# First self-attention's weight transposes ahead of the next rows, and six sign-MLP tiles split ahead of the last rows

## The chip, the core and the metric

The kernel runs on one core of a Trainium2 chip. The core has a matrix engine (TensorE, PE in the rows; PEld is its weight load), a vector engine (VectorE, DVE), a scalar engine (ScalarE, ACT), a general engine (GpSimd, POOL) and a queue that issues transfers (SyncE, SP). The engines run side by side and wait for one another by semaphores. The metric is the device time of one launch in microseconds, the median of several executions.

## What is computed

The reference takes x of 16 x 64 rows by 512 and runs two layers of three blocks, each block on the layer norm of x and added to it. Only the two blocks that the change touches are shown, cut to what matters.

```python
def _L0_attn_ref(x, Wq, bq, Wk, bk, Wv, bv, Wp):        # 16 heads of 32, groups of 64 tokens
    q = (x @ Wq + bq).reshape(Bb, Nn, H, D)
    k = (x @ Wk + bk).reshape(Bb, Nn, H, D)
    v = (x @ Wv + bv).reshape(Bb, Nn, H, D)
    q = jnp.einsum('bnhe,ei->bnhi', q, Wp)
    k = jnp.einsum('bnhe,ei->bnhi', k, Wp)
    scores = jnp.einsum('bnhi,bmhi->bnhm', q, k) / math.sqrt(D)
    attn = jax.nn.softmax(scores, axis=-1)
    return jnp.einsum('bnhm,bmhe->bnhe', attn, v).reshape(Bb, Nn, E)
...
def _L0_ffn_ref(x, k0, k1, k2, s0, s1, s2):             # weights are +1 or -1
    h = jnp.concatenate([x, -x], axis=-1)
    h = jax.nn.relu(s0 * _conn_dense(k0, h)) * 2        # 512 (as 1024) -> 2048
    h = jax.nn.relu(s1 * _conn_dense(k1, h)) * 2        # 2048 -> 2048
    return s2 * _conn_dense(k2, h)                      # 2048 -> 512
...
x = x + _L0_attn_ref(_layernorm(x, axis=-1), ...)
x = x + _L0_ffn_ref(_layernorm(x, axis=-1), ...)
```

## The kernel before

Every engine has its own program, written out by hand in the order in which it runs; nothing reorders it. A wait at the head of an engine's queue holds all that stands behind it there.

**First self-attention** (`head_attention`). The 1024 rows are eight tiles of 128. A turn handles two tiles (256 rows), so there are four turns, i = 0 to 3; the turns 1 and 2 are the body of a hardware loop, 0 and 3 are written apart. In turn i TensorE does in this order: the key projections and the query projections (`project_transposed`, three products of high and low halves: hi by hi, lo by hi, hi by lo; L941), scores of the first tile (L957), transposes of the rows that the sign MLP will read (`transpose_signs`, L932), values of the first tile (L948), scores of the second tile, values of the second tile, transposes of the next turn's normalised rows (`transpose_x`, L925), then for the softmax weights four batches of four transposes (`transpose_weights(i, s, n)`, tile s, half n of the heads, L966) with the weighted values (`attend`, L976) of tile 0 after the third batch and those of tile 1 after the fourth.

Around them: ScalarE takes the exponentials out of the score banks (`exponentials(i, s, n)`, eight activations of 64 columns each, L1033), copies the transposed next rows (`copy_x`, L1027, x_xT_hi) and the first tile's values (L1067). VectorE takes the negative maxima (L1104, s_nmax), copies the second tile's values (L1171, s_v_diag), copies the transposed weights out of their two banks (`copy_weights`, L1109, s_pT), makes the low half of the next rows (`split_x`, L1099, x_xT_lo), scales and adds the result (`attended`, L1113, L1116, L1121), and takes the statistics of rows. The weight transposes write the banks 4 and 5, the same as the key projections and the sign transposes; a batch for tile 1 waits until the batch of tile 0 in the same bank was copied (`pT_ok`). The next turn's projection waits for both halves of the next rows (`xhi_ok`, `xlo_ok`). VectorE also expands one chunk of the sign MLP's first weights in each turn (L1152), and GpSimd adds the output bias to the rows in the same stretch (L1230).

**Sign MLP.** The rows go in two halves of 512. In the first layer TensorE makes 16 hidden tiles of 128 x 512, eight matmuls each (L2079), into two banks in turn. ScalarE takes each through the ReLU (L2124) into one of two float32 buffers, and VectorE splits a buffer into its float16 high half (L2178) and low half (L2180) (`split_hidden`). ScalarE's tile n waits until tile n-2 is split; TensorE's tile n waits until ScalarE has read tile n-2. The first half of the rows comes from the turns 0 and 1. The last two row tiles (turn 3) are normalised here: VectorE aggregates the statistics (L2130), GpSimd makes the reciprocal deviation (L2217, L2219), VectorE makes f_xn (L2134), and TensorE transposes them after the whole first layer of the first half (L2087). GpSimd expands the second layer's weights (L2227, f_w), one piece after hidden tiles 3, 7, 11 and 15 and later one for each tile.

## Time and profile before

| what | value |
|---|---|
| three executions | 1104.45, 1107.32 and 1108.89 us, median 1107.32 |
| the profiled execution, its own time | 1112.53 us |
| its span in the trace | 1110.7 us |
| TensorE busy, share of the span | 1066.0 us, 96% |
| VectorE, ScalarE, GpSimd | 58%, 31%, 19% |
| mean granted clock of TensorE | 0.985 |
| first self-attention, turns 0 to 3 | 176.3 to 291.4 us |
| sign MLP, first layer of the first half | 291.4 to 324 us |

Times in the rows are from the span's start. A timeline row gives start, duration, engine, line, operation, output and inputs, the form, how many instructions of a kind stand in a row (x8: from the first's start to the last's end), and in brackets the engine's idle time before with what released it. A matmul's end is modelled, so a row of TensorE can overlap the next. Where the row ends an idle time in "issue", the engine waited for nothing that the profile shows.

### The profile page before, as it was taken

How to read it: one execution, taken by the hardware profiler on the slowest of the kernel's cores; microseconds unless marked ns; L12 is line 12 of the kernel's file. 1: busy time of each engine (PE TensorE's matmuls, PEld its weight loads, DVE VectorE, ACT ScalarE, POOL GpSimd, SP SyncE). 2: the span in 40 equal slices, each digit the busy share in tenths (PEclk: the TensorE clock that was granted, in tenths of full speed). 3: DMA queues.
4: the chain of work that ended last, by engine and by line, in shares of the span. 5: the costliest groups of instructions: out<-in, count | busy, mean ns of one | idle time of the engine just before them, and what ended most of it. 6: DMA issues, size and time to landing. Idle time of an engine off the chain costs nothing.

```text
span 1110.7 us, 16819 instructions
## 1 busy us (share of the span) xinstructions
PE 1066.0 (96%) x6165; PEld 664.2 (60%) x6165; DVE 641.2 (58%) x1114; ACT 347.2 (31%) x984; POOL 208.9 (19%) x202
## 2 busy tenths in 40 slices
PE   7999989999899999999999999999889999999897
PEld 4566648888444444444444466657679687887433
DVE  2454345787666732256762174457865947569677
ACT  1232235666530000130001042236232514225534
POOL 0111101333122222000001611132414122140002
PEclk9999989999999999999999999999999999999898
DMA  9976902000024591014536469963000000021105
GB/s 338 387 255 219 354 20 76 2 1 23 26 93 146 177 19 20 0 53 155 179 119 222 168 217 372 366 240 113 1 1 1 1 0 0 1 108 59 58 1 76
DMA packets 68593, 129.59 MB, mean 117 GB/s; under 512 B 9408, under 2 KB 13504, under 8 KB 68160
## 3 DMA queue, kind: packets, MB, share of 16 engines
q1 hardware_dynamic: 67680, 127.38, 35.2%
q0 software_dynamic: 864, 1.57, 1.1%
q8 instruction: 29, 0.48, 0.2%
q14 instruction: 20, 0.16, 0.0%
HBM read 120.92 MB, written 8.01 MB: 116 GB/s over the span
## 4 chain that ended last, share of the span: by engine, by line
PE 72%; issue 11%; DVE 8%; POOL 4%; SPq 2%; DMA 2%; ACT 1%; POOLq 0%; DVEq 0%; ACTq 0%
PE bank L2079 24%; PE bank L449 5%; PE bank L2106 5%; PE bank L419 4%; PE bank L941 4%; PE bank L380 3%; PE bank L2307 3%; PE bank L948 2%; PE bank L1562 2%; PE bank L1631 2%; PE bank L2342 2%; PE bank L494 2%; PE bank L483 2%; PE bank L469 2%; DMA xres<-in_x_dram 2%
## 5 line engine op out<-in xcount | busy, mean ns | idle before, releaser
L2124 ACT ACTIVATE f_act<-bank,f_sgn 128x512 f32<-128x512 f32 x64 | 44.0, 687 | 267.8 <-PE bank L2079 262.2
L2079 PE MATMUL bank<-f_a_lo,f_w 128*128 128x512 f16 x512 | 115.7, 379 | 0.0
L2079 PE MATMUL bank<-f_a_hi,f_w 128*128 128x512 f16 x512 | 115.7, 379 | 0.0
L2079 PEld LDWEIGHTS bank<-f_a_lo,f_w 128*128 x512 | 50.1, 98 | 60.4
L2079 PEld LDWEIGHTS bank<-f_a_hi,f_w 128*128 x512 | 50.1, 98 | 60.2
L2178 DVE CAST f_b_hi<-f_act 128x512 f16<-128x512 f32 x32 | 28.4, 887 | 95.0 <-ACT f_act L2124 85.6
L1838 DVE TENSOR_TENSOR s_e<-s_pair,s_tables 128x512 f32<-128x512 f32 x64 | 41.4, 689 | 42.8 <-POOL s_kT L1914 15.4
L419 PE MATMUL bank<-x_cT,x_qT 128*64 128x512 f32 x256 | 62.9, 637 | 0.0
L449 PE MATMUL bank<-x_cN,x_eT 128*64 128x512 f32 x256 | 56.9, 596 | 0.0
L1823 DVE TENSOR_TENSOR s_k_diag<-s_kT,s_spread 128x512 f32<-128x512 f32 x64 | 48.8, 819 | 1.6 <-PE bank L1587 1.6
L1720 ACT ACTIVATE s_e<-bank,s_nmax 128x64 f32<-128x64 f32 x128 | 38.1, 338 | 35.5 <-DVE s_nmax L1783 35.4
L2227 POOL TENSOR_SCALAR f_w<-f_upper_bits 128x2048 bf16<-128x2048 uint8 x16 | 30.9, 1932 | 82.1 <-PE bank L2079 82.1
L711 DVE TENSOR_TENSOR x_aT_lo<-bank,x_aT_hi 128x512 fp32r<-128x512 f32 x16 | 11.1, 692 | 60.8 <-ACT x_aT_hi L574 60.8
L744 POOL TENSOR_TENSOR x_mv<-x_mv,eps 128x2 f32<-128x2 f32 x10 | 1.9, 194 | 214.9 <-DVE x_mv L606 214.9
L1033 ACT ACTIVATE s_e<-bank,s_nmax 128x64 f32<-128x64 f32 x128 | 38.3, 351 | 4.1 <-DVE s_nmax L1104 4.0
L1587 PE MATMUL bank<-s_k_diag,s_qT 128*64 128x256 f32 x256 | 34.2, 401 | 4.8 <-DVE s_k_diag L1823 4.0
L419 PEld LDWEIGHTS bank<-x_cT,x_qT 128*64 128x64 f32 x256 | 18.0, 145 | 34.6 <-issue 34.3
L449 PEld LDWEIGHTS bank<-x_cN,x_eT 128*64 128x64 f32 x256 | 17.6, 137 | 32.8 <-issue 32.6
L2079 PE MATMUL bank<-f_xT_hi,f_w 128*128 128x512 f16 x128 | 33.8, 387 | 3.2 <-ACT f_act L2124 3.2
L1913 POOL TENSOR_TENSOR s_kT<-s_e 128x256 f32<-128x256 f32 x16 | 13.3, 831 | 115.8 <-DVE s_e L1838 115.8
L390 PE MATMUL bank<-x_kw,x_qw 128*128 128x512 f32 x64 | 30.5, 637 | 4.2 <-DMA x_kw<-in_x_kw_dram 4.2
L751 POOL MEMSET x_ones<- 128x128 f32 x1 | 0.2, 205 | 180.6 <-DMA x_bk<-in_x_kb_dram 180.6
(339 smaller groups left out, 2300.2 us busy)
## 6 DMA issues: line engine op xcount, KB each, us to landing
x_cT<-in_ctx_cols_dram SPq DMA_DIRECT2D x32, 1024.0 KB, 8.9
x_cN<-in_ctx_rows_dram SPq DMA_DIRECT2D x32, 1024.0 KB, 11.5
f_upper_bits<-in_f_w_dram SPq DMA_DIRECT2D x20, 256.0 KB, 3.9
f_row<-in_f_wg_dram SPq DMA_DIRECT2D x11, 256.0 KB, 3.7
f_long_row<-in_f_wd_dram SPq DMA_DIRECT2D x4, 704.0 KB, 6.2
f_row<-in_f_wu_dram SPq DMA_DIRECT2D x11, 256.0 KB, 2.7
f_part<-in_f_wgT_dram SPq DMA_DIRECT2D x8, 352.0 KB, 3.4
f_part<-in_f_wuT_dram SPq DMA_DIRECT2D x8, 352.0 KB, 3.3
```

The lines of the kernel that those rows point to most:

```text
L380: mm = pe.matmul(bank[Q_BANK[half]][:, a * PT:(a + 1) * PT], l[:, k, c * P:(c + 1) * P], r[:, k, :], start=(m == 0 and k == 0), stop=(m == ...
L419: mm = pe.matmul(bank[S_BANK[s]][SEQ * b:SEQ * (b + 1), :], qT[:, k, tokens], cT[s][:, b, k, :], start=(k == 0), stop=(k == KC - 1))
L449: mm = pe.matmul(bank[AV_BANK[s]][SEQ * b:SEQ * (b + 1), :], eT[s][:, k, SEQ * b:SEQ * (b + 1)], cN[s][:, b, k, :], start=(k == 0), stop=( ...
L941: mm = pe.matmul(bank[banks[g]][:, a * PT:(a + 1) * PT], l[:, k, c * P:(c + 1) * P], r[:, k, :], start=(m == 0 and k == 0), stop=(m == 2 a ...
L1033: ins = act.activation(e_sb[s][n][:, j * SEQ:(j + 1) * SEQ], bank[S_BANK[s][n]][:, j * SEQ:(j + 1) * SEQ], ACT.Exp, bias=nmax[s][:, h:h + ...
L1587: mm = pe.matmul(at[SEQ * b:SEQ * (b + 1), cols], qT[:, g, a, tokens], k_diag[g % 2][:, a, b, :], start=False, stop=(a == AB - 1), skip_gr ...
L1720: ins = act.activation(e_sb[n][:, j * SEQ:(j + 1) * SEQ], bank[S_BANK[s][n]][:, j * SEQ:(j + 1) * SEQ], ACT.Exp, bias=nmax[s][:, h:h + 1], ...
L1823: ins = dve.tensor_tensor(k_diag[g % 2][:, a, :, :].rearrange("p b (j n) -> p b j n", j=4), kT[:, g, a, s * P:(s + 1) * P].rearrange("p (b ...
L1838: ins = dve.tensor_tensor(flat(prods[t]), flat(pair[:, :, :]), table(t), ALU.mult)
L2079: mm = pe.matmul(h_bank[s][:, :], weights(2 * i + s, k), part[:, k, cols], start=(n == 0 and k == 0), stop=(n == 1 and k == k_chunks - 1))
L2106: mm = pe.matmul(y_bank[t % 2][:, :], part[:, k, t * P:(t + 1) * P], w2_sb[:, k, :], start=(n == 0 and k == 0), stop=(n == 1 and k == HC - 1))
L2124: act.activation(act32[s][:, :], h_bank[s][:, :], ACT.Relu, scale=sgn[:, layer % 2:layer % 2 + 1]).then_inc(h_read, 1)
```

## The change

In the first self-attention, TensorE transposes tile 0's weights (two batches) before it transposes the next turn's rows; the wait for the low half of the rows (`xlo_ok`) moves from the head of the key projection to its third product. ScalarE does the second tile's second half of exponentials before it copies the next rows. VectorE copies tile 0's two weight batches before the second tile's values, and all four batches before it splits the next rows. In the sign MLP, VectorE splits the first six hidden tiles of the first half before it normalises the last two row tiles; the loop over the tiles then begins at pair 3. Each engine runs as many instructions of each kind as before, apart from the loop's own.

```diff
-            def project_transposed(banks, hi, lo, done):
+            def project_transposed(banks, hi, lo, done, split=None):
                 for g in range(2):
                     for a in range(2):
                         c = 2 * g + a
                         for m, (l, r) in enumerate(((hi, xT_hi), (lo, xT_hi), (hi, xT_lo))):
+                            if split is not None and c == 0 and m == 2:
+                                pe.wait_ge(xlo_ok, split)
                             for k in range(KC):
...
                 pe.wait_ge(xhi_ok, 2 * (FIRST + i) + 2)
-                pe.wait_ge(xlo_ok, 2 * (FIRST + i) + 2)
-                project_transposed(K_BANK, wk_hi, wk_lo, k_done)
+                project_transposed(K_BANK, wk_hi, wk_lo, k_done, 2 * (FIRST + i) + 2)
                 project_transposed(Q_BANK, wq_hi, wq_lo, q_done)
...
                 project_values(1)
-                if not last:
-                    pe.wait_ge(e_ok, 4 * i + 2)
-                    transpose_x(i + 1)
                 if not first:
                     pe.wait_ge(flo_ok, 2 * i)
                 transpose_weights(i, 0, 0)
                 transpose_weights(i, 0, 1)
+                if not last:
+                    pe.wait_ge(e_ok, 4 * i + 2)
+                    transpose_x(i + 1)
                 transpose_weights(i, 1, 0)
...
                 exponentials(i, 1, 0)
+                exponentials(i, 1, 1)
                 if not last:
                     copy_x(i + 1)
-                exponentials(i, 1, 1)
...
                 negative_maxima(i, 1, 1)
+                copy_weights(i, 0, 0)
+                copy_weights(i, 0, 1)
                 dve.wait_ge(v_done, 2 * i + 2)
...
                 ins.then_inc(v1_ok, 1)
-                copy_weights(i, 0, 0)
-                copy_weights(i, 0, 1)
                 copy_weights(i, 1, 0)
+                copy_weights(i, 1, 1)
                 if not last:
                     split_x(i + 1)
-                copy_weights(i, 1, 1)
                 attended(i, 0)
...
-            dve.wait_ge(rstd_ok, 2)
-            for s in range(2):
-                dve.tensor_scalar(xn[s][:, :], xres[:, TILES - 2 + s, :], mv[:, s, 0:1], rstd[:, s:s + 1],
-                                  ALU.subtract, ALU.mult).then_inc(xn_ok, 1)
+            def normalise_last():
+                dve.wait_ge(rstd_ok, 2)
+                for s in range(2):
+                    dve.tensor_scalar(xn[s][:, :], xres[:, TILES - 2 + s, :], mv[:, s, 0:1], rstd[:, s:s + 1],
+                                      ALU.subtract, ALU.mult).then_inc(xn_ok, 1)
...
-                        with dve.Fori(0, HC // 2) as i:
+                        ahead = 0
+                        if half == 0:
+
+                            ahead = 3
+                            for n in range(2 * ahead):
+                                split_hidden(first, n, n % 2, hi, lo)
+                            normalise_last()
+                        with dve.Fori(ahead, HC // 2) as i:
```

What stands in a row on VectorE at the end of turn 0 (turns 1 and 2 alike), before:

```order
L1104 TENSOR_REDUCE s_nmax<-bank 128x8 x2
L1171 COPY s_v_diag<-bank 64x8x32 x4
L1109 COPY s_pT<-bank 128x512 x3
L1099 TENSOR_TENSOR x_xT_lo<-bank,x_xT_hi 128x4x128 x2
L1109 COPY s_pT<-bank 128x512
L1113 RECIPROCAL s_total<-s_total 128x16
```

And after:

```order
L1105 TENSOR_REDUCE s_nmax<-bank 128x8 x2
L1110 COPY s_pT<-bank 128x512 x2
L1174 COPY s_v_diag<-bank 64x8x32 x4
L1110 COPY s_pT<-bank 128x512 x2
L1100 TENSOR_TENSOR x_xT_lo<-bank,x_xT_hi 128x4x128 x2
L1114 RECIPROCAL s_total<-s_total 128x16
```

Two weight copies moved ahead of the values' copies, and the low halves moved behind the last weight copy.

TensorE at the end of turn 0, from the second tile's values on, before:

```order
L948 MATMUL bank<-x_m_hi,x_xT_lo 128x512 x4
L925 MATMUL bank<-ident,x_xn 128x128 x8
L966 MATMUL bank<-ident,s_e 128x128 x12
L976 MATMUL bank<-s_v_diag,s_pT 64x64 x16
L966 MATMUL bank<-ident,s_e 128x128 x4
L976 MATMUL bank<-s_v_diag,s_pT 64x64 x16
```

And after:

```order
L950 MATMUL bank<-x_m_hi,x_xT_lo 128x512 x4
L968 MATMUL bank<-ident,s_e 128x128 x8
L925 MATMUL bank<-ident,x_xn 128x128 x8
L968 MATMUL bank<-ident,s_e 128x128 x4
L978 MATMUL bank<-s_v_diag,s_pT 64x64 x16
L968 MATMUL bank<-ident,s_e 128x128 x4
L978 MATMUL bank<-s_v_diag,s_pT 64x64 x16
```

The eight transposes of tile 0's weights stand ahead of the eight of the next rows.

VectorE at the start of the sign MLP, before:

```order
L2130 BN_AGGR f_mv<-stats 128x2 x2
L2134 TENSOR_SCALAR f_xn<-xres,f_mv,f_rstd 128x512 x2
L2201 UNCONDITIONAL_BRANCH
L2201 ISA
L2178 ISA
L2178 COPY f_a_hi<-f_act 128x512
```

And after (the pair of rows at L2180 and L2182 stands there six times; one is shown):

```order
L2131 BN_AGGR f_mv<-stats 128x2 x2
L2180 CAST f_a_hi<-f_act 128x512
L2182 TENSOR_TENSOR f_a_lo<-f_act,f_a_hi 128x512
...
L2136 TENSOR_SCALAR f_xn<-xres,f_mv,f_rstd 128x512 x2
L2210 UNCONDITIONAL_BRANCH
L2210 ISA
L2180 ISA
```

The two row tiles f_xn moved behind six splits, which now stand outside the loop.

## Rows read from the trace of the kernel before

**Rows 1.** Windows: stretch, length, busy times of PE PEld DVE ACT POOL, clock, DMA.
```profile
233.50:262.50 29.00, 27.87 (x252) 23.54 (x248) 23.40 (x46) 18.39 (x84) 10.44 (x8) 1.00 0.00 0
...
291.40:324.00 32.60, 29.41 (x132) 12.97 (x129) 24.53 (x42) 10.31 (x15) 8.26 (x6) 0.95 0.10 24
...
303.00:304.00 1.00, 1.00 (x4) 0.36 (x3) 0.88 (x3) 0.00 (x0) 0.00 (x0) 0.50 0.00 0
```

**Rows 2.** Timeline, all engines, end of turn 2 and start of turn 3.
```profile
256.08 1.73 DVE L1171 COPY s_v_diag<-bank 64x256 f32<-64x256 f32 x4 [1.29 <-PE bank L948]
...
256.92 1.11 ACT L1027 CAST x_xT_hi<-bank 128x512 fp32r<-128x512 f32 x2
257.85 1.29 DVE L1109 COPY s_pT<-bank 128x512 f32<-128x512 f32 x2
...
259.90 0.42 ACT L1033 ACTIVATE s_e<-bank,s_nmax 128x64 f32<-128x64 f32 x1
259.96 1.28 DVE L1099 TENSOR_TENSOR x_xT_lo<-bank,x_xT_hi 128x512 fp32r<-128x512 f32 x2
...
260.46 0.42 PEld L966 LDWEIGHTS bank<-ident,s_e 128*128 128x128 f32 x4 [0.21 <-ACT s_e L1033]
...
261.16 0.69 DVE L1109 COPY s_pT<-bank 128x512 f32<-128x512 f32 x1
...
262.52 0.54 PEld L941 LDWEIGHTS bank<-x_xT_hi,s_wk_hi 128*128 128x128 f32 x4
```

**Rows 3.** Timeline, the middle of turn 2, where VectorE and GpSimd meet.
```profile
243.33 4.57 POOL L1230 TENSOR_TENSOR xres<-xres,s_out_bias 128x512 f32<-128x512 f32 x2
243.48 3.29 DVE L1152 TENSOR_TENSOR f_w<-f_upper_bits,f_lower_bits  x1
...
246.69 1.39 DVE L1104 TENSOR_REDUCE s_nmax<-bank 128x8 f32<-128x512 f32 x2
...
247.40 0.32 ACT L1033 ACTIVATE s_e<-bank,s_nmax 128x64 f32<-128x64 f32 x1 [1.20 <-DVE s_nmax L1104]
```

**Rows 4.** Timeline, end of turn 0: the transposes' issue and the last weight copy.
```profile
197.73 1.02 PEld L925 LDWEIGHTS bank<-ident,x_xn 128*128 128x128 f32 x8
...
203.23 0.68 DVE L1109 COPY s_pT<-bank 128x512 f32<-128x512 f32 x1
```

**Rows 5.** Timeline, end of turn 3.
```profile
285.14 1.73 DVE L1171 COPY s_v_diag<-bank 64x256 f32<-64x256 f32 x4 [1.37 <-PE bank L948]
...
288.14 1.28 ACT L2112 ACT_TABLE_LOAD   x1
...
290.08 0.69 DVE L1109 COPY s_pT<-bank 128x512 f32<-128x512 f32 x1 [0.98 <-PE bank L966]
```

**Rows 6.** Timeline, first layer of the sign MLP, from its start to its end.
```profile
291.44 0.55 PEld L2079 LDWEIGHTS bank<-f_xT_hi,f_w 128*128 x4
...
295.71 0.25 DVE L2130 BATCH_NORM_AGGREGATE f_mv<-stats 128x2 f32<-128x6 f32 x2 [0.24 <-DVE stats L1184]
...
297.01 1.90 POOL L2227 TENSOR_SCALAR f_w<-f_upper_bits 128x2048 bf16<-128x2048 uint8 x1
297.06 2.58 DVE L2134 TENSOR_SCALAR f_xn<-xres,f_mv,f_rstd 128x512 f32<-128x512 f32 x2 [1.11 <-POOL f_rstd L2219]
...
...
300.10 0.69 DVE L2180 TENSOR_TENSOR f_a_lo<-f_act,f_a_hi 128x512 f32 x1
...
300.89 0.69 ACT L2124 ACTIVATE f_act<-bank,f_sgn 128x512 f32<-128x512 f32 x1 [5.09 <-DVE f_a_lo L2180]
...
301.71 1.03 PE L2079 MATMUL bank<-f_xT_hi,f_w 128*128 128x512 f16 x4 [3.19 <-ACT f_act L2124]
...
323.91 1.01 PEld L2087 LDWEIGHTS bank<-ident,f_xn 128*128 128x128 f32 x8
```

**Rows 7.** Timeline, turn 1: a short GpSimd operation with VectorE operations beside it.
```profile
209.18 0.15 DVE L1131 TENSOR_TENSOR s_s_abs<-s_s_abs,f_scales_in 128x2 f32<-128x2 f32 x1
209.24 0.69 POOL L1213 TENSOR_TENSOR s_fmv<-s_fmv,minus_half 128x2 f32<-128x2 f32 x1
```

## The prediction, made before the changed kernel ran

> **What bounds the kernel now.** I read the windows first, then the timeline of the places that the diff touches. TensorE is the bound in both blocks, so only its idle time and its clock can be won. In a middle turn of the attention it is busy 27.87 of 29.00 us at full clock [rows 1]: about 1.1 us a turn are idle, nearly all at the turn's end. In the first layer of the sign MLP it is busy 29.41 of 32.60 us and the mean granted clock is 0.95 [rows 1], so there it loses idle time and clock.
>
> The end of a turn is a relay [rows 2]. ScalarE copies the next rows at 256.92, and only then takes the last eight exponentials, which end with 259.90 + 0.42 = 260.32. TensorE's fourth batch of weight transposes waits for them (260.46), VectorE's last weight copy follows at 261.16, which is 0.70 after that batch was issued, and the next turn begins at 262.52, which is 1.36 after the copy's start. So the last exponential sets the end of turn 2. What sets the exponentials is VectorE: TensorE's scores wait for a maximum at 246.69 that stands behind the 3.29 us expansion, and ScalarE idled 1.20 us for it [rows 3]. The loop is VectorE, ScalarE, TensorE, VectorE, and TensorE's own work is only just inside it.
>
> At the MLP's start TensorE issues tiles from 291.44 and stops after four, since VectorE's first split comes behind the two f_xn, which end at 297.06 + 2.58 = 299.64; it goes on at 301.71 after 3.19 us idle [rows 6].
>
> **The attention, part by part.** No instruction is added or removed; only the order moves, and no transfer moves with it.
>
> ScalarE: the exponentials of tile 1, second half, go ahead of the row copies. The last exponential then ends earlier by the time of the copies. They last 1.11 us as a pair, and the next operation begins some 0.95 after their start, so 0.95 us.
>
> VectorE: the low halves (1.28 us [rows 2]) go behind the last weight copy. That copy comes earlier, but what follows it, `attended`, statistics, k_diag and the maxima, begins 1.28 us after it instead of at once. So in each turn of the loop ScalarE gives back 0.95 and VectorE takes 1.28: the loop is longer by 0.33 us. The gain is one of the relay, and it shrinks from turn to turn.
>
> Turn 0: TensorE issues the weight transposes at 197.73 in place of the rows' transposes [rows 4]. The first copy can begin 0.70 later, 198.43. VectorE then does two weight copies (1.29), four value copies (1.73) and the third weight copy (0.62 to the next), with some 0.1 between: the last begins at 202.17, where it began at 203.23 [rows 4]. Shift -1.05. VectorE's work behind it: -1.05 + 1.28 = +0.23.
> Turn 1: ScalarE starts +0.23, the last exponential is at +0.23 - 0.95 = -0.72; TensorE's own order was the last there before by about 0.1 to 0.2, so the copy shifts by about -0.85, and VectorE behind it by +0.43.
> Turn 2: the same: +0.43 - 0.95 = -0.52. VectorE behind it +0.76, but in turn 3 it takes no statistics for a next turn, and it waits there for TensorE's key projection, so this is absorbed.
> Turn 3: the values' copy waited for TensorE at 285.14; all shifts by -0.52, to 284.62. The exponentials end before the table load at 288.14 [rows 5], now 287.62. VectorE's chain is then two weight copies, four value copies, the third weight copy: from about 284.9, 1.29 + 1.73 + 0.62 + 0.1 = 288.6 for the last copy, where it began at 290.08 [rows 5]. Shift -1.48. Everything behind it, TensorE's start of the MLP and VectorE's statistics of the last rows, shifts with it.
>
> The wait moved into the key projection: TensorE reaches it three quarters through the first of four column groups, two products of four matmuls after the start, about 0.94 us. The low halves are ready 0.62 + 1.28 = 1.90 after the last copy's start, TensorE is there 1.36 + 0.94 = 2.30 after it: 0.4 us of slack. What queues behind that wait is the whole projection, and k_diag on both other engines waits for it. The trace has no such wait in the middle of a stream; bounds are 0 and 0.2 us a turn (next to the 0.21 us idle at 260.46 [rows 2]). In turns 1 and 2 the loop hides it; I take 0.1 for each of turns 0 and 3. The attention gives -1.48 + 0.2 = -1.3 us, with ends -1.6 and -0.9.
>
> **The sign MLP.** What is there to win: after the stall 12 tiles take 301.71 to 323.91 = 22.2 us; 5% of 32.60 us lost to clock is 1.6 us, so 20.6 / 12 = 1.72 us a tile. Sixteen tiles are 27.5 us, and 323.91 - 291.44 = 32.47 [rows 6]. The stretch holds 4.9 us of loss: 3.3 idle and 1.6 at the lower of the two clocks (1.2 against 2.4 GHz), which stood at 0.50 at 303 us, right behind that idle time [rows 1].
>
> What stays: VectorE's statistics end at 295.96. A split takes about 1.2 us (from the end of f_xn, 299.64, to the subtraction's end, 300.79), ScalarE follows 0.10 later for 0.69, TensorE 0.13 later [rows 6]. Tile 0 is split at 297.2, ScalarE is done at 298.0, TensorE's tile 4 can start at 298.1; it is due at 291.44 + 4 x 1.72 = 298.3. No stall. Tile 1: its cast would begin at 297.2, but GpSimd begins its 1.90 us expansion at 297.01. The f_xn pair that began at 297.06 ended 0.73 after that expansion [rows 6]; in rows 3 both engines' operations are long by what the other one took: the two exclude each other there. So the cast ends some 0.3 us after 298.91, the subtraction at 300.0, ScalarE at 300.8, TensorE's tile 5 at 300.9 where it is due at 300.05: a stall of 0.8 us. Behind it VectorE needs 1.2 us a tile against 1.72 and catches up. The stall is shorter than those in the attention's turns, where the clock stayed at 1.00 [rows 1], so I charge no clock for it.
>
> f_xn now stands after tile 5, about 12.5 us into the layer, and GpSimd's second expansion falls there too, so up to 2.58 us [rows 6] go before tile 6 is split. TensorE's tile 10 needs tile 8's activation, which needs tile 6 split: due at 17.2 us from the start, ready at 12.5 + 2.6 + 1.2 + 0.1 + 0.69 + 0.13 = 17.2. It just holds; cover gone, it costs what is over. The transposes of f_xn come at 27.5 us, so no wait there. The MLP gives 4.9 - 0.8 = 4.1 us, with ends 3.0 and 4.9.
>
> A rule bears on this. A 0.69 us GpSimd operation ran while VectorE's two-input operation beside it took 0.15 us [rows 7]: short ones do not exclude each other noticeably. The Trainium skill (SBUF — State Buffer, "SBUF: two separate sides") says that whichever of a GpSimd operation and a VectorE operation in a two-port mode or with two SBUF inputs starts first holds the shared pair for the whole instruction and the other is blocked. The trace agrees for the 1.90 us expansion and for rows 3, not for those of [rows 7].
>
> **Sum.** -1.3 - 4.1 = -5.4 us. From the profiled execution's own 1112.53 that gives 1107.1; it lies 5.2 us above the median, which I put down to the execution, so the forecast for the median is 1107.32 - 5.4 = **1101.9 us**. Transfers and later stages are released by TensorE's progress and shift along.
>
> **The rivals.**
> *Nothing held (1101.1).* GpSimd's short operations are themselves pushed back by VectorE's splits, the expansion begins after tile 3's split, and no stall is left: -1.3 - 4.9 = -6.2. For it: the margin between 297.01 and 297.2 is small.
> *Held longer (1103.0).* The short GpSimd operations after the statistics hold VectorE too, so that the expansion lies behind tile 1's cast and ahead of its subtraction: 298.4 + 1.9 + 0.7 = 301.0, ScalarE 301.8, tile 5 at 301.9, a stall of 1.9 us; -1.3 - 3.0 = -4.3. This is what the Trainium skill's rule (same page and section) would make of it. Against it: [rows 7].
> *The loop eats the attention's gain (1103.2).* If VectorE sets every turn from the first, turns 0 to 2 cost 3 x 0.33 = 1.0 instead, which cancels the 1.0 that turn 3 alone gives (1.48 - 0.52): 0 - 4.1. For it: ScalarE's 1.20 us wait in rows 3. Against: turn 0 has slack.
> *The stall only moves (1106.1).* f_xn behind tile 5 stops TensorE at tile 10 for 2.6 us and the clock falls again for 1.6: the MLP gives 4.9 - 0.8 - 4.2 = -0.1 at best; -1.3 + 0.1 = -1.2. For it: the 17.2 against 17.2.
> *Slower (1108.2).* The moved wait: if the low halves come over 0.4 us later than reckoned, TensorE stops a second time within 2 us at each turn's start, and the clock falls there as it did in the MLP. With 0.5 us more in each of three turns and 1.6 for each fall, 6.3 us, against 5.4: +0.9. It decides once all three turns lose the clock and at least 0.2 us each. Against it: the 0.4 slack, and 1.1 us of idle a turn left the clock at 1.00.
> That the change does not do what it says is ruled out by the order of the engines' queues.
>
> **How the numbers follow.** Forecast 0.42 (its own range 1101.0 to 1103.0), nothing held 0.15, loop 0.15, held longer 0.12, stall moves 0.08, slower 0.05, others 0.03. The range 1099.4 to 1104.9 holds the first four with 1.6 us for the spread of the executions on either side. A measurement of this kernel can tell about 0.5%, 5.5 us, from no change: 1101.8. The forecast lies just short of it, so a good third of its chance and most of "nothing held" go to faster: 0.40; same 0.55; slower 0.05.
>
> **What would show it.** In the profile after: the first layer of the MLP takes 28 to 29 us from its start to the transposes, with a clock of 1.00; TensorE's wait for f_act of about 0.8 us instead of 3.2; the third turn starts at 262.0 and the MLP at about 290.1 on the same scale; maxima in turn 2 come 0.4 us later than 246.69, not earlier. It would be wrong if the MLP's stall were over 1.5 us or the clock fell in it, or if the MLP began at or after 291.4.

## The result, and the profile after

The changed kernel takes 1101.36 us (median of six, 1099.77 to 1101.90) against 1107.59 us for the kernel before (median of six, 1103.41 to 1108.89). The medians differ by 6.2 us, a ratio of 0.9944. The ratio estimated from the executions is 0.9932, 95% interval 0.9913 to 0.9950, which is 5.5 to 9.6 us: faster, clear of no change, and past the 1101.8 us that the prediction had set as its bound, though a gain of 0.6% is small. The forecast was 1101.9 us.

The two profiled executions differ by more, 1110.7 against 1100.1 us of span, and this has to be taken apart first. The code ahead of the attention is the same in both, yet the attention begins at 176.35 us before and at 173.5 after, and in the eleven experiments below it begins between 171.3 and 175.4. In the profile before, TensorE waited 2.40 us for a transfer at 142.97 us, and behind that its granted clock stood at 0.50:

```profile
142.97 0.80 PE L118 MATMUL bank<-s_wpT 128*128 128x128 f32 x2 [2.40 <-DMA s_out_bias<-in_s_bv_dram]
...
145.00:148.00 3.00, 3.00 (x8) 0.71 (x6) 0.00 (x0) 0.00 (x0) 0.00 (x0) 0.50 0.00 0
```

(The first row is from the timeline, the second from the windows.) From the end of that wait to the attention it took 33.38 us, where the changed kernel and the eleven experiments, with the clock at 1.00 there, took 30.26 to 30.32. So everything is measured inside its stretch. Marking each turn by the first weight load of its key projection, and the layer's end by the first weight load of the transposes of f_xn, the traces give:

| us | turn 0 | turn 1 | turn 2 | turn 3 | attention | first MLP layer |
|---|---|---|---|---|---|---|
| before | 28.23 | 28.97 | 28.97 | 28.92 | 115.09 | 32.47 |
| after | 27.17 | 29.00 | 29.22 | 27.97 | 113.36 | 27.83 |
| difference | -1.06 | +0.03 | +0.25 | -0.95 | -1.73 | -4.64 |

Together -6.37 us, close to the 6.2 between the medians. From the layer's end to the end of the span it is 786.8 before and 785.4 after, and 783.9 to 787.8 in the experiments. That too is the clock in the main, as the last section shows.

The windows of after. They answer to [rows 1]; the columns are those of [rows 1], the first a middle turn, the second the first MLP layer:

```profile
230.00:258.90 28.90, 27.55 (x248) 23.24 (x246) 22.97 (x46) 18.38 (x84) 10.45 (x8) 1.00 0.00 0
...
286.90:314.70 27.80, 27.73 (x130) 12.41 (x128) 25.03 (x42) 10.31 (x15) 8.83 (x6) 1.00 0.10 29
```

TensorE is now busy 27.73 of 27.80 us in the layer at full clock. The middle turn has kept its idle time and a little more: 1.35 us of 28.90, where it was 1.13 of 29.00.

The timeline of after at the end of turn 2 answers to [rows 2]:

```profile
256.62 1.16 ACT L1028 CAST x_xT_hi<-bank 128x512 fp32r<-128x512 f32 x2
...
257.56 0.69 DVE L1110 COPY s_pT<-bank 128x512 f32<-128x512 f32 x1 [1.23 <-PE bank L968]
258.17 1.28 DVE L1100 TENSOR_TENSOR x_xT_lo<-bank,x_xT_hi 128x512 fp32r<-128x512 f32 x2
...
259.36 0.24 DVE L1114 RECIPROCAL s_total<-s_total 128x16 f32<-128x16 f32 x1
```

ScalarE's row copies now follow the exponentials, the last weight copy waits 1.23 us for TensorE's fourth batch, and VectorE's division (L1114) begins 1.80 us after that copy's start, where the same division of the kernel before (its L1113, at 261.77) began 0.61 after its copy's start at 261.16 [rows 2]. That is the pair of low halves, pushed into the loop: 1.28 us long, with 1.19 from its start to the division's. The middle of turn 2 answers to [rows 3]:

```profile
240.71 4.58 POOL L1231 TENSOR_TENSOR xres<-xres,s_out_bias 128x512 f32<-128x512 f32 x2
...
240.86 3.28 DVE L1153 TENSOR_TENSOR f_w<-f_upper_bits,f_lower_bits  x1
...
244.06 1.27 DVE L1105 TENSOR_REDUCE s_nmax<-bank 128x8 f32<-128x512 f32 x2
```

Against the turn's start (229.70) the maxima come at 14.36 us, against 13.14 us before. In turn 1 they come at 14.15 against 12.96. In the turns 0 and 3 they stay at 12.84.

And the start of the MLP's first layer, which begins at 286.89, answers to [rows 6]:

```profile
291.16 0.25 DVE L2131 BATCH_NORM_AGGREGATE f_mv<-stats 128x2 f32<-128x6 f32 x2 [0.24 <-DVE stats L1185]
...
291.33 0.39 DVE L2180 CAST f_a_hi<-f_act 128x512 f16<-128x512 f32 x1
291.49 0.28 POOL L2226 TENSOR_TENSOR f_var<-f_mv,eps 128x2 f32<-128x2 f32 x1 [18.14 <-DVE f_mv L2131]
291.76 0.69 DVE L2182 TENSOR_TENSOR f_a_lo<-f_act,f_a_hi 128x512 f16<-128x512 f32 x1
291.85 1.17 POOL L2228 TENSOR_TENSOR f_rstd<-f_var,minus_half 128x2 f32<-128x2 f32 x1
...
292.36 0.42 DVE L2180 CAST f_a_hi<-f_act 128x512 f16<-128x512 f32 x1
...
292.82 0.69 DVE L2182 TENSOR_TENSOR f_a_lo<-f_act,f_a_hi 128x512 f16<-128x512 f32 x1
...
293.01 2.26 POOL L2236 TENSOR_SCALAR f_w<-f_upper_bits 128x2048 bf16<-128x2048 uint8 x1
293.43 2.12 DVE L2180 CAST f_a_hi<-f_act 128x512 f16<-128x512 f32 x1
...
295.58 0.69 DVE L2182 TENSOR_TENSOR f_a_lo<-f_act,f_a_hi 128x512 f16<-128x512 f32 x1
...
296.37 0.69 ACT L2125 ACTIVATE f_act<-bank,f_sgn 128x512 f32<-128x512 f32 x1 [1.67 <-DVE f_a_lo L2182]
...
299.38 2.57 DVE L2136 TENSOR_SCALAR f_xn<-xres,f_mv,f_rstd 128x512 f32<-128x512 f32 x2
```

VectorE splits right behind the statistics. GpSimd's short operations are the ones that are pushed: 0.28 and 1.17 us where they took 0.20 and 0.72 before (L2217 and L2219 in the same place), so its expansion begins 6.12 us into the layer and not 5.57, beside the subtraction of the second split, which takes its usual 0.69 us. The third cast, which begins beside the expansion, takes 2.12 us in place of 0.42, and there VectorE has the time: ScalarE waits 1.67 us, TensorE does not.

The pair f_xn is slow as well (2.57 us, beside the second expansion), and this is not hidden entirely. A short idle time does not show in brackets, since a matmul's modelled end lies behind the next one's start; the starts show it. Four matmuls take 0.86 to 0.87 us from start to start. At tile 10 it is 1.10, at tile 13 it is 1.02:

```profile
302.79 0.69 DVE L2182 TENSOR_TENSOR f_a_lo<-f_act,f_a_hi 128x512 f32 x1 [0.50 <-DVE f_a_hi L2180]
...
303.31 1.03 PE L2080 MATMUL bank<-f_xT_lo,f_w 128*128 128x512 f16 x4
...
304.41 1.03 PE L2080 MATMUL bank<-f_xT_hi,f_w 128*128 128x512 f16 x4
...
305.28 1.03 PE L2080 MATMUL bank<-f_xT_lo,f_w 128*128 128x512 f16 x4
...
306.41 2.42 DVE L2182 TENSOR_TENSOR f_a_lo<-f_act,f_a_hi 128x512 f32 x1
...
308.73 1.03 PE L2080 MATMUL bank<-f_xT_lo,f_w 128*128 128x512 f16 x4
...
309.75 1.03 PE L2080 MATMUL bank<-f_xT_hi,f_w 128*128 128x512 f16 x4
```

So the changed layer loses 0.24 us at tile 10, behind f_xn and a first subtraction in the loop that waits 0.50 us for its cast, and 0.15 us at tile 13, behind a subtraction that the third expansion (306.39) holds. Without any loss the 128 matmuls of the layer take 27.65 us from start to start, 27.43 by the table's marker, which lies 0.22 us before the transposes' first matmul. By the same count the layer before lost 3.35 us in its stall and 1.69 to the clock.

### The profile page after: what moved, and what is told of

Same layout as the page of the kernel before. It is cut to its first block, busy times and chain, and to the rows that moved or that the text cites. A ratio compares the mean times of both kernels' runs of the same rounds, so it can differ in the third digit from the quotient of the medians.

```text
span 1100.1 us, 16786 instructions
## 1 busy us (share of the span) xinstructions
PE 1059.1 (96%) x6165; PEld 662.1 (60%) x6165; DVE 641.7 (58%) x1114; ACT 347.1 (32%) x984; POOL 208.8 (19%) x202
## 4 chain that ended last, share of the span: by engine, by line
PE 68%; issue 11%; DVE 9%; POOL 4%; ACT 3%; SPq 2%; DMA 2%; DVEq 0%; POOLq 0%; ACTq 0%
PE bank L2080 25%; PE bank L449 5%; PE bank L2107 5%; PE bank L419 4%; PE bank L380 3%; PE bank L2316 3%; PE bank L943 2%; PE bank L1563 2%; PE bank L1632 2%; PE bank L2351 2%; ACT s_e L1034 2%; PE bank L494 2%; PE bank L483 2%; PE bank L469 2%; DMA xres<-in_x_dram 2%
## 5 line engine op out<-in xcount | busy, mean ns | idle before, releaser
L2180 DVE CAST f_b_hi<-f_act 128x512 f16<-128x512 f32 x32 | 27.0, 845 | 94.8 <-ACT f_act L2125 94.8
L419 PE MATMUL bank<-x_cT,x_qT 128*64 128x512 f32 x256 | 59.4, 606 | 0.0
L419 PEld LDWEIGHTS bank<-x_cT,x_qT 128*64 128x64 f32 x256 | 17.2, 139 | 32.0 <-issue 31.6
L2216 DVE SCALAR_TENSOR_TENSOR xres<-bank,f_out_scale,xres 128x512 f32<-128x512 f32 x8 | 6.0, 751 | 47.0 <-PE bank L2107 47.0
```

Of the source, the lines that this page charges most:

```text
L419: mm = pe.matmul(bank[S_BANK[s]][SEQ * b:SEQ * (b + 1), :], qT[:, k, tokens], cT[s][:, b, k, :], start=(k == 0), stop=(k == KC - 1))
```

## The experiments

Each kernel ran beside the kernel before on its chip, and the ratios are to that kernel. Executions of one kernel scatter by some 2 us, so the ratios decide little under 3 us. The verdicts rest on the stretches of the traces: turns and layers with the same code and the clock at 1.00 repeat to 0.05 us.

| run | ratio, 95% interval | turns 0 to 3, us | attention | first layer |
|---|---|---|---|---|
| e1 | 0.9971 (0.9958 to 0.9984) | 27.16, 29.00, 29.20, 28.00 | 113.36 | 33.68 |
| e2 | 0.9945 (0.9925 to 0.9966) | 28.23, 29.01, 28.96, 28.91 | 115.11 | 27.82 |
| e3 | 0.9968 (0.9950 to 0.9987) | 28.22, 28.98, 28.96, 28.91 | 115.07 | 29.83 |
| e4 | 0.9912 (0.9889 to 0.9934) | 27.16, 27.87, 27.89, 27.97 | 110.89 | 27.84 |
| e5 | 0.9949 (0.9933 to 0.9966) | 27.80, 29.00, 29.20, 27.97 | 113.97 | 27.82 |
| e6 | 0.9939 (0.9920 to 0.9959) | 28.36, 29.07, 29.06, 27.99 | 114.48 | 27.82 |
| e7 | 0.9948 (0.9931 to 0.9964) | 27.15, 28.96, 29.17, 27.97 | 113.25 | 28.43 |
| e8 | 0.9967 (0.9953 to 0.9982) | 27.17, 29.00, 29.21, 27.99 | 113.37 | 30.64 |
| e9 | 0.9981 (0.9961 to 1.0000) | 28.23, 28.98, 28.95, 28.92 | 115.08 | 32.48 |
| e10 | 0.9980 (0.9955 to 1.0005) | 28.68, 30.07, 30.99, 29.26 | 119.00 | 27.84 |
| e11 | 0.9951 (0.9929 to 0.9974) | 27.17, 29.01, 29.22, 27.99 | 113.39 | 28.22 |

### The two parts apart: e1 and e2

e1 is the changed kernel with this undone:

```diff
-                        ahead = 0
-                        if half == 0:
...
-                            normalise_last()
-                        with dve.Fori(ahead, HC // 2) as i:
+                        with dve.Fori(0, HC // 2) as i:
```

> The attention part of the change alone; the sign MLP as before. Theory: the two parts add up and do not touch each other. The traces of before and after give the attention 1.7 us (176.35 to 291.44 against 173.5 to 286.89), so this kernel is 1.7 us faster than before (1.2 to 2.2), the first layer of the MLP still takes about 32.5 us, with TensorE idle 3.2 us and the clock down behind it. Rival (the loop of VectorE and ScalarE eats it): 0 us. Rival (the parts need each other): over 3 us or a loss.

e2 is the kernel before with only that part made.

> The MLP part alone; the attention as before. Theory: the first layer falls from 32.5 to 27.8 us, 4.6 us faster than before (3.6 to 5.2), TensorE's wait gone and the clock at 1.00 through the layer. Rival (the stall moves to tile 10 behind f_xn): about 1 us. Rival (most of the difference between the two profiles was chance in other stages): under 3 us.

The parts add up: -1.73 us in e1's attention, -4.65 in e2's layer, each to 0.02 us what the full change has there. In e1 the stall of 3.19 us stood in the layer and the clock was down behind it; here it took a larger bite than in the profile before, 33.68 us against 32.47. The windows of e1:

```profile
288.07:321.80 33.73, 30.54 (x132) 13.20 (x129) 24.45 (x42) 10.31 (x15) 8.22 (x6) 0.90 0.09 23
298.30:300.00 1.70, 1.65 (x4) 0.66 (x5) 1.58 (x4) 0.69 (x1) 0.00 (x0) 0.50 0.00 0
...
303.00:304.00 1.00, 1.00 (x4) 0.43 (x3) 0.88 (x2) 0.00 (x0) 0.00 (x0) 0.50 0.00 0
```

So against the changed kernel's layer the same stall costs 4.6 us in one execution and 5.9 in another. By the matmuls' starts it is 3.35 us of stall in both, and 1.7 and 2.9 us of clock.

### What made the stall long: e3

```diff
                 if f < 4:
-                    pool.wait_ge(h_done, 4 * f + 3)
+                    pool.wait_ge(h_done, 4 * f + 3 if f else 6)
```

> The kernel before, with one number changed: GpSimd's first expansion of the second layer's weights waits for hidden tile 6 in place of tile 3, so that it no longer runs beside f_xn. Theory (the two engines exclude each other for the length of the instruction): the f_xn pair takes 1.0 us in place of 2.58, TensorE's idle time falls from 3.2 to 1.6 us, and if so short an idle time leaves the clock up, the kernel is 3.2 us faster than before, else 1.6. Rival (f_xn is slow for another reason): f_xn stays 2.6 us, no difference.

The timeline of e3, the same place as [rows 6]:

```profile
296.04 1.00 DVE L2134 TENSOR_SCALAR f_xn<-xres,f_mv,f_rstd 128x512 f32<-128x512 f32 x2 [1.10 <-POOL f_rstd L2219]
...
299.12 1.03 PE L2079 MATMUL bank<-f_xT_hi,f_w 128*128 128x512 f16 x4 [1.61 <-ACT f_act L2124]
...
302.84 4.07 POOL L2227 TENSOR_SCALAR f_w<-f_upper_bits 128x2048 bf16<-128x2048 uint8 x2 [6.83 <-PE bank L2079]
...
308.37 1.04 PE L2079 MATMUL bank<-f_xT_hi,f_w 128*128 128x512 f16 x4 [0.44 <-ACT f_act L2124]
```

And its windows, the layer first:

```profile
290.40:320.30 29.90, 27.84 (x132) 12.50 (x129) 24.26 (x42) 10.30 (x15) 8.35 (x6) 1.00 0.10 26
...
301.00:304.00 3.00, 3.00 (x16) 1.37 (x14) 2.17 (x4) 1.37 (x2) 1.16 (x1) 1.00 0.00 0
```

f_xn takes 1.00 us once the expansion is out of its way, the idle time is halved and the clock stays up. The layer falls by 2.64 us, less than the 3.2 written beforehand: the first two expansions now run one behind the other (4.07 us), a subtraction beside the second takes 2.16 us in place of 0.69, and TensorE stops once more, for 0.44 us at tile 9. One number on GpSimd gives over half of what the reorder gives in this layer. The rival is out: f_xn was slow through the other engine alone.

### The loop of the middle turns: e4, e9, e5

e4 (on the changed kernel) and e9 (on the kernel before) make the same edit:

```diff
                 _, upper, lower, expanded, _ = sign_weights
-                dve.wait_ge(bits_in, 32)
-                dve.tensor_tensor(expanded[:, i, :], upper[:, i, :], lower[:, i, :], ALU.subtract).then_inc(sign_ok, 1)
                 negative_maxima(i, 0, 0)
                 negative_maxima(i, 0, 1)
                 if not last:
                     normalise_x(2 * i + 2, i + 1)
+                dve.wait_ge(bits_in, 32)
+                dve.tensor_tensor(expanded[:, i, :], upper[:, i, :], lower[:, i, :], ALU.subtract).then_inc(sign_ok, 1)
```

> The changed kernel, and in each turn VectorE expands the sign weights after the next rows are normalised in place of before the first maxima. Theory (the turns 1 and 2 are a loop VectorE, ScalarE, TensorE, set by maxima that stand behind the expansion): the maxima of turn 2 come 1.3 us earlier against the turn's start, ScalarE does not wait 1.2 us for them, each of the turns 1 and 2 gets about 1 us shorter, 2 us faster than the changed kernel (8.2 faster than before; 7 to 9.5). Rival (TensorE's own order sets the turns): no difference to the changed kernel, 6.2 faster than before.

> The kernel before, with only the expansion of the sign weights moved behind the normalisation, as in e4. Theory: before, the maxima of the turns 1 and 2 came 0.12 and 0.30 us later than they could (12.96 and 13.14 against 12.84 us after the turn's start), so the loop was only just closed; both turns get 0.1 to 0.3 us shorter, the attention 0.4 us in all. The 2.5 us of e4 are to be had only where the reorder has pushed the maxima to 14.15 and 14.36. Rival (the expansion is a cost of its own whatever the order): 2 us and more, as in e4.

The timeline of e4 in turn 2, which began at 226.35:

```profile
239.20 0.69 DVE L1105 TENSOR_REDUCE s_nmax<-bank 128x8 f32<-128x512 f32 x1 [1.59 <-PE bank L959]
...
239.93 0.32 ACT L1034 ACTIVATE s_e<-bank,s_nmax 128x64 f32<-128x64 f32 x1 [0.91 <-DVE s_nmax L1105]
```

The maxima are back at 12.85 us, VectorE itself waits 1.59 us for TensorE, and the turns 1 and 2 fall to 27.87 and 27.89: 2.47 us off the attention of the changed kernel, 4.20 off that before. The same edit on the kernel before moved its maxima to 12.84 too and its attention by 0.01 us, where 0.4 had been expected. So the expansion costs nothing in the old order and 2.5 us in the new one. The change itself closed the loop; before, the end of the turn set the turns, and the wait in [rows 3] had cover. At its new place the expansion no longer meets GpSimd's addition: it takes 2.29 us and the addition's pair 2.51, where they took 3.28 and 4.58 beside each other. e4 beats both kernels: 1099.27 us (median of six), where the kernel before took 1109.27 on that chip. Its interval overlaps the changed kernel's, and the two were not timed side by side; that it is faster than the changed kernel rests on the 2.47 us in the trace.

e5 puts the moved wait back:

```diff
+                pe.wait_ge(xlo_ok, 2 * (FIRST + i) + 2)
-                project_transposed(K_BANK, wk_hi, wk_lo, k_done, 2 * (FIRST + i) + 2)
+                project_transposed(K_BANK, wk_hi, wk_lo, k_done)
```

> The changed kernel with the wait for the low halves back at the head of the key projection. Theory: in the changed order the low halves are ready 1.9 us after the last weight copy began, the projection could start 1.36 after it, so each of the three turn starts is 0.55 us later: 1.6 us slower than the changed kernel, 4.6 faster than before. Rival (the low halves are ready anyway, the moved wait is for nothing): same as the changed kernel, 6.2 faster than before.

```profile
201.75 0.71 PE L943 MATMUL bank<-x_xT_hi,s_wk_hi 128*128 128x256 f32 x4 [0.60 <-DVE x_xT_lo L1101]
```

TensorE's wait of 0.60 us is there as reckoned, but only turn 0 is longer, by 0.63; the turns 1 and 2 stay at 29.00 and 29.20, and 1.6 was expected. It is the loop again: what starts TensorE later there does not move VectorE's maxima (they come 0.64 us sooner after a start that is 0.64 later). The expectation forgot what the prediction had said, that the loop hides this in the turns 1 and 2.

### The order inside the relay: e6 and e10

```diff
                 copy_weights(i, 1, 0)
-                copy_weights(i, 1, 1)
                 if not last:
                     split_x(i + 1)
+                copy_weights(i, 1, 1)
```

> The changed kernel with VectorE's low halves back ahead of the last weight copy. ScalarE copies the rows only after its last exponential, so VectorE waits for those copies (1.1 us) and then splits (1.3 us) before the copy. Theory: the last copy comes about 1.7 us later in each of three turns; VectorE's work behind it no longer loses the 1.3 us of the split but the whole relay is later: 3 to 5 us slower than the changed kernel, 1 to 3 faster than before. Rival (where the split stands is all one, since VectorE does the same work in each turn): within 1 us of the changed kernel.

```profile
257.18 1.28 DVE L1100 TENSOR_TENSOR x_xT_lo<-bank,x_xT_hi 128x512 fp32r<-128x512 f32 x2
...
258.38 0.68 DVE L1110 COPY s_pT<-bank 128x512 f32<-128x512 f32 x1
...
259.11 0.69 PE L978 MATMUL bank<-s_v_diag,s_pT 128*64 128x64 f32 x16 [1.01 <-DVE s_pT L1110]
```

Turn 0 loses 1.19 us; the turns 1 and 2 together change by -0.09, and 3 to 5 us were expected in all. The two ends of the trade are seen at once: the last weights wait for the split (TensorE idles 1.01 us for their copy), and since the low halves are no longer behind it, the maxima come at 12.96 and 13.17. In the middle turns the one pays for the other. The size of the wait was overrated too: half of the low halves is made while ScalarE still copies the other tile.

e10 undoes ScalarE's order alone:

```diff
                 exponentials(i, 1, 0)
-                exponentials(i, 1, 1)
                 if not last:
                     copy_x(i + 1)
+                exponentials(i, 1, 1)
```

> The changed kernel with ScalarE's row copies back ahead of its last exponentials; VectorE and TensorE keep the changed order. Theory (the loop gives ScalarE's 0.95 us and takes VectorE's 1.28): turn 0 gets 0.6 us longer than in the changed kernel (27.8), the turns 1 and 2 take 1.28 us more than before where the maxima set them, 30.0 to 30.3 us each, turn 3 stays 28.0; the attention 2.5 to 3.5 us longer than in the changed kernel, longer than before. Rival (VectorE's order alone makes the gain): within 0.3 us of the changed kernel.

```profile
258.43 1.07 ACT L1028 CAST x_xT_hi<-bank 128x512 fp32r<-128x512 f32 x2 [0.56 <-PE bank L925]
...
261.93 0.66 PE L968 MATMUL bank<-ident,s_e 128*128 128x128 f32 x4 [1.59 <-ACT s_e L1034]
```

And two windows, one at the start of turn 2 and one at the start of turn 3:

```profile
233.00:236.00 3.00, 3.00 (x21) 2.88 (x16) 2.75 (x7) 0.00 (x0) 0.00 (x0) 0.50 0.00 0
264.00:267.00 3.00, 3.00 (x19) 2.88 (x16) 2.75 (x6) 0.00 (x0) 0.00 (x0) 0.50 0.00 0
```

The attention takes 119.00 us, 3.9 more than before and 5.6 more than in the changed kernel, past the expected 3.5. TensorE waits 1.59 to 1.60 us for the last exponentials in each of the turns 0, 1 and 2, in the turns 0 and 2 also because ScalarE's copies wait for transposes that TensorE does later (0.85 and 0.56 us). Behind the second and the third of these waits the clock fell to 0.50: TensorE is busy 29.23 us in turn 2 and 28.22 in turn 3, where the changed kernel has 27.87 and 26.93 for the same work. That is 2.65 us, and without it the attention would be some 3.0 us longer than in the changed kernel, inside the expected 2.5 to 3.5, and 1.3 longer than before. So the direction is the theory's, and the extra is the clock. The profiled execution is also the longest of its ten (1110.82 us, median 1106.89); whether the others lost the clock there is not shown. VectorE's and TensorE's reorder without ScalarE's is a loss in the attention.

### Where f_xn may stand: e7 and e8

e7 has `ahead = 1` (two tiles), e8 `ahead = HC // 2` (all sixteen, without the loop).

> The changed kernel with two tiles split ahead of f_xn in place of six. Theory: tiles 0 and 1 are done at about 5.9 us into the layer, f_xn then runs beside GpSimd's expansion (up to 2.6 us) and tile 2 is split at about 10 us, where TensorE's tile 6 needs it by 9.4: a stall of 0.5 to 1.5 us, no fall of the clock, 1 us slower than the changed kernel. Rival (any split ahead of f_xn is enough): same as the changed kernel.

> The changed kernel with all sixteen tiles split ahead of f_xn. Theory: TensorE's transposes of f_xn stand right behind the layer, and the sixteenth tile is split some 2 us after TensorE made it, so they wait for the split and for f_xn: 2.5 to 3.5 us slower than the changed kernel, more if the clock falls. Rival (f_xn has slack everywhere): same.

```profile
297.49 1.03 PE L2080 MATMUL bank<-f_xT_hi,f_w 128*128 128x512 f16 x4 [0.64 <-ACT f_act L2125]
```

```profile
317.32 1.11 PE L2088 MATMUL bank<-ident,f_xn 128*128 128x128 f32 x8 [2.84 <-DVE f_xn L2136]
```

The first row is e7's stall at tile 6, 0.64 us, with f_xn held for 2.57 us by the expansion; its layer is 0.60 us longer than the changed kernel's. The second is e8's, at the transposes: 2.8 us longer, and the clock stayed at 1.00. Both came out in place; e8's in size too, and e7's stall inside its range, though the layer lost 0.6 us where 1 was written. Six tiles are past the first hazard, at the price of the 0.24 us at tile 10, and far from the second.

### The missing stall: e11

```diff
-            pool.wait_ge(var_ok, 2)
...
-            pool.tensor_tensor(rstd[:, :], var[:, :], core.minus_half[:, 0:1].to_broadcast([P, 2]), ALU.pow).then_inc(rstd_ok, 1)
             for f in range(HC):
...
                 pool.tensor_scalar(w1_sb[:, f, :, :], raw[f % RAW].rearrange("p (k f) -> p k f", k=HC), 2.0, -1.0,
                                    ALU.mult, ALU.add).then_inc(w1_ok, 1)
+                if f == 0:
+                    pool.wait_ge(var_ok, 2)
...
+                    pool.tensor_tensor(rstd[:, :], var[:, :], core.minus_half[:, 0:1].to_broadcast([P, 2]), ALU.pow).then_inc(rstd_ok, 1)
```

> The changed kernel, and GpSimd makes its first expansion of the second layer's weights ahead of the reciprocal deviation of the last rows in place of behind it, so about 0.6 us earlier, at 5.5 us into the layer, where VectorE's second cast stands. Theory (my forecast's 0.8 us of stall failed only since VectorE's first split pushed GpSimd back): the second split is held by 1.9 us, TensorE stalls 0.5 to 1 us at its sixth tile, the layer takes 28.3 to 28.8 us. Rival (VectorE is far enough ahead for any place of the expansion): 27.8 us as in the changed kernel.

```profile
293.31 2.19 POOL L2232 TENSOR_SCALAR f_w<-f_upper_bits 128x2048 bf16<-128x2048 uint8 x1 [19.02 <-PE bank L2080]
...
293.78 2.26 DVE L2182 TENSOR_TENSOR f_a_lo<-f_act,f_a_hi 128x512 f16<-128x512 f32 x1
...
296.96 1.03 PE L2080 MATMUL bank<-f_xT_hi,f_w 128*128 128x512 f16 x4 [0.29 <-ACT f_act L2125]
```

This layer began at 287.86, so the expansion begins 5.45 us into it. It lets the second cast through and holds the second subtraction, which takes 2.26 us in place of 0.69. TensorE stops at its sixth tile for 0.29 us and the layer takes 28.22 us, 0.4 more; 0.5 to 1 and 28.3 to 28.8 were expected, so both fall just short. That is the mechanism of the forecast's stall at its place, at half its size; the changed kernel is free of it through 0.7 us in GpSimd's timing.

## Where the prediction was right and where not

**The sum** said -5.4 us, and the stretches give -6.37. 1101.36 lies inside the range, 0.5 us from the forecast. The parts are off by more, both to the same side (0.4 us in the attention, 0.5 in the layer); that the medians agree better is in part luck, for the six executions before have a median 0.3 us above that of the three the forecast started from. It went to "faster", to which 0.40 was given, against 0.55 for "same": the forecast lay 0.1 us short of the bound, so this was near a toss.

**Turns 0 and 3.** -1.05 was reckoned for turn 0, -1.06 is measured; for turn 3 by itself 1.48 - 0.52 = 0.96 was reckoned, 0.95 is measured. The count of VectorE's copies from the transposes' landing was the right chain in both.

**Turns 1 and 2.** The mechanism was right: the gain of a turn is ScalarE's 0.95, its price VectorE's 1.28, and the turns grow. The sizes were +0.20 and +0.33, measured are +0.03 and +0.25. The step that was too pessimistic is "So the last exponential sets the end of turn 2". In [rows 2] VectorE's last weight copy has no idle time before it; it begins at 261.16 right behind the low halves, so VectorE's own chain ended there as well. In e9 the maxima come 0.1 and 0.3 us sooner and the turns stay as long: in the old order they had that much cover, and the first part of the loss went into it. The rival "the loop eats the attention's gain" is out, e4 shows what it is worth all the same: 2.5 us.

**The moved wait** was charged at 0.1 us in each of two turns. Turn 0 came out at its reckoned length without it: it costs nothing that can be seen. e5 shows that it is worth 0.6 us. This and the turns' 0.25 us make up the difference between -1.3 and -1.73, just outside the ends given (-1.6 and -0.9).

**The MLP layer** was forecast at -4.1 and is -4.64. The mechanism was right; two terms of the sum were off, with opposite signs. What is to win had been sized at 4.9 us and is 5.04 by the matmuls' starts (3.35 of stall and 1.69 of clock), so that term was good. The stall of 0.8 us at tile 5 did not come: the step "GpSimd begins its 1.90 us expansion at 297.01" was taken over from before, though the change puts VectorE's splits beside the two short GpSimd operations ahead of it. VectorE was also ahead of the reckoning: a split outside the loop takes 1.03 us from cast to cast, where 1.2 had been taken, so the second cast begins 5.47 us into the layer and not 5.76. e11 shows the stall where the expansion is earlier. And 0.39 us were lost where nothing had been charged, at the tiles 10 and 13. The rival "nothing held" named GpSimd's delay and had 0.15; its case came true with differences: the expansion begins beside the second split already, the third cast and later a subtraction are held, and the 0.39 us are left.

**f_xn at tile 10.** 12.5 us into the layer and 2.58 us were reckoned; f_xn came at 12.49 for 2.57. The prediction said that it just holds, 17.2 against 17.2. Tile 10 began at 17.51, 0.24 us late, since the first split behind f_xn took 1.53 us (301.95 to 303.48) and not 1.2. So the rival "the stall only moves" named a real place, at a tenth of its size and without a fall of the clock. "Slower" is out: the clock is 1.00 in all turns of the changed kernel. But what stood against it, that 1.1 us of idle a turn left the clock up, is a narrow margin: in e10 1.6 us did not.

**The signs.** On the scale of the profile before, the third turn was to start at 262.0 and the MLP at 290.1; they start at 261.7 and 289.7. The maxima of turn 2 come 0.2 us later than 246.69, not 0.4. The layer was to take 28 to 29 us and takes 27.83.

**The Trainium skill's rule** (SBUF — State Buffer, "SBUF: two separate sides": whichever starts first holds the shared pair, the other is blocked) stands better than [rows 7] let it look. There VectorE's operation begins first, 0.06 us ahead of GpSimd's, so by the rule it would not have been held at all, and its usual 0.15 us say nothing against the rule. In the profile after, VectorE's first subtraction begins at 291.76, GpSimd's power operation at 291.85, and it is the GpSimd operation that is held, 1.17 us in place of 0.72; in e11 the expansion begins first and VectorE's subtraction takes 2.26 us in place of 0.69. The forecast had drawn from [rows 7] that short operations do not matter, and did not ask in which direction. In one direction this holds in the trace: the cast at 292.36 and the subtraction at 292.82 begin while the power operation is under way and take their usual 0.42 and 0.69 us, which the rule by itself would not give.

## What to carry to other kernels

When work moves behind the last step of a relay, add up the whole loop, not the step: what one engine is relieved of and another is given decides the middle turns, and an operation that had cover there (the expansion) may have to move along. An engine's start time taken from the old trace is good only where nothing new stands beside what comes before it. And a stall is worth its idle time plus whatever the clock does behind it, so halving it can give more than half, as in e3; but a short stall is no safe one, as e10 shows.

## What the runs showed of the hardware

TensorE's clock fell from 2.4 to 1.2 GHz (granted 0.50) behind the idle time of 3.19 us in all three profiles that had it there (the kernel before, e1 and e9), and cost 1.7, 2.9 and 1.7 us. The length of the idle time alone does not tell whether it falls. It stayed at 1.00 behind 2.84 us (e8) and behind 1.61 (e3), and of e10's three idle times of 1.6 us it stayed behind the first and fell behind the other two, which cost 1.4 and 1.3 us.

An exclusion between VectorE and GpSimd shows in whichever operation came second: f_xn 2.58 us against 1.00, the expansion on GpSimd 2.26 against 1.90 to 2.05, the short power operation 1.17 against 0.72, a subtraction with two SBUF inputs 2.26 against 0.69, a cast 2.12 against 0.42. Some hundredths of a microsecond between two starts do not decide it: in e11 the second cast begins 0.02 us behind the expansion's start and takes its usual 0.42.

Outside the compared stretches the profiles differ by the clock too. TensorE waits 1.94 us at one place some 0.8 ms into every profile (820.66 us before, 811.69 after). Behind it the clock fell in eight of the thirteen profiles, the kernel before among them, and from there to the next such wait it took 212.9 us; in the five where it stayed up (after, e3, e7, e8 and e11) it took 211.3 to 211.4. These five have the shortest rest of the program behind the layer, 783.9 to 785.5 us against 786.2 to 787.8. So of the 10.6 us between the two profiled executions, 3.1 and 1.6 are a clock that one lost and the other kept in code that the change does not touch. Why it falls in one execution and not in the next stays open.
